# Attention kernel on Trainium2: the inversion of a tile's softmax normalisers moves from VectorE to GpSimd

## What is computed

```python
q = _fq_sym(q, axis=-1); k = _fq_sym(k, axis=-1); v = _fq_sym(v, axis=2)
attn = jnp.einsum('bhqd,bhkd->bhqk', q, k)
attn = jax.nn.softmax(attn.astype(jnp.float32), axis=-1)
attn = _fq_unsigned(attn, axis=-1)      # to 0..255 of the row's largest
out = jnp.einsum('bhqk,bhkd->bhqd', attn, v)
out = out @ Wp + bp
```

## Time and profile before

| what | value |
|---|---|
| median of three runs | 1166.4 us |
| the profiled execution's own time | 1166.14 us |
| its span | 1164.4 us |
| mean granted TensorE clock | 0.994 |
| busy in the span: PE, DVE, ACT, POOL | 90%, 82%, 77%, 60% |
| attention in its steady form | about 130 to 690 us of the span |
| finish of tile 0 and of tile 15 on VectorE | at 136.8 and at 732.7 us |

### The profile page before, as it was taken

How to read it: one execution, slowest core, us unless ns; L and a number is a source line. 1 busy time by engine, 2 the same in 40 slices (tenths; PEclk the granted TensorE clock), 3 DMA queues, 4 the chain that set the end, 5 groups by cost and what they waited for, 6 DMA issues and landing times.

```text
span 1164.4 us, 24047 instructions
## 1 busy us (share of the span) xinstructions
PE 1048.7 (90%) x8281; PEld 606.3 (52%) x8396; DVE 950.6 (82%) x1748; ACT 891.8 (77%) x1546; POOL 701.3 (60%) x625
## 2 busy tenths in 40 slices
PE   8988888888888888888888889899998999999997
PEld 4743444444444444444444447656654465557775
DVE  6999999999999999999999996863336788953335
ACT  4779999999999999999999996734543576834441
POOL 3016888888777878888788776447651000753332
PEclk9999999999999999999999999899999999999999
DMA  6697998888888889888876764856938001523336
GB/s 193 120 163 149 173 172 162 169 169 171 167 172 175 165 166 170 178 162 170 155 118 111 115 109 78 243 170 181 321 115 331 0 1 46 178 84 109 97 97 233
DMA packets 388799, 176.36 MB, mean 151 GB/s; under 512 B 330413, under 2 KB 373650, under 8 KB 388680
## 3 DMA queue, kind: packets, MB, share of 16 engines
q1 hardware_dynamic: 381976, 157.85, 62.1%
q0 software_dynamic: 6480, 16.77, 4.3%
q10 hardware_dynamic: 224, 0.20, 0.1%
HBM read 52.70 MB, written 43.59 MB: 83 GB/s over the span
## 4 chain that ended last, share of the span: by engine, by line
PE 49%; DVE 28%; ACT 13%; issue 5%; DMA 2%; POOL 2%; SPq 1%; ACTq 0%; POOLq 0%; DVEq 0%
DVE top L426 22%; ACT weight L485 10%; PE bank L220 8%; PE bank L234 8%; PE bank L1187 4%; PE bank L2616 4%; PE bank L1580 3%; PE bank L252 3%; PE bank L2632 3%; PE bank L1166 2%; PE bank L1174 2%; PE bank L1853 1%; PE bank L1598 1%; PE bank L682 1%; POOL dispatched_rows L1823 1%
## 5 line engine op out<-in xcount | busy, mean ns | idle before, releaser
L485 ACT ACTIVATE weight<-bank,bias,sq_all 128x1024 uint8<-128x1024 f32 x512 | 609.9, 1201 | 24.0 <-PE bank L234 18.7
L426 DVE TENSOR_REDUCE top<-bank 128x1 f32<-128x512 f32 (+1 forms) x683 | 610.2, 951 | 11.5 <-PE bank L220 1.1
L537 POOL CAST weight<-turned 128x2048 bf16<-128x2048 uint8 x256 | 478.8, 1892 | 41.0 <-PE bank L252 22.2
L234 PE MATMUL bank<-kT,query 128*128 128x512 bf16 x917 | 284.1, 382 | 26.4 <-ACT weight L485 12.2
L252 PEld LDWEIGHTS bank<-v_sb,weight 128*128 128x128 bf16 x4096 | 172.0, 96 | 102.7 <-POOL weight L537 0.5
L220 PE MATMUL bank<-kT,qspace 64*128 64x512 bf16 x687 | 135.0, 387 | 55.8 <-DVE top L426 55.8
L252 PE MATMUL bank<-v_sb,weight 128*128 128x16 bf16 x4096 | 172.6, 170 | 0.8 <-POOL weight L537 0.4
L220 PE MATMUL bank<-kT,query 128*128 128x512 bf16 x329 | 124.8, 379 | 2.1 <-DVE top L426 1.4
L234 PEld LDWEIGHTS bank<-kT,query 128*128 128x128 bf16 x1024 | 59.9, 97 | 103.9 <-ACT weight L485 61.9
L1823 POOL DMA_INDIRECT dispatched_rows<-qspace,put x32 | 37.1, 1160 | 116.0 <-DVE qspace L2373 106.9
L485 ACT ACTIVATION_READ_ACCUMULATOR weight<-bank,bias,sq_all 128x1 f32 x512 | 101.7, 199 | 0.0
(11 more groups left out here) (352 smaller groups left out, 1471.7 us busy)
## 6 DMA issues: line engine op xcount, KB each, us to landing
dispatched_rows<-zeros SPq DMA_DIRECT2D x32, 524.0 KB, 3.1
answered_rows<-zeros SPq DMA_DIRECT2D x16, 512.0 KB, 3.2
late<-answered_rows SPq DMA_DIRECT2D x16, 512.0 KB, 6.3
erow<-dispatched_rows SPq DMA_DIRECT2D x39, 131.0 KB, 2.1
wgu<-in_L_ffn_w_gate SPq DMA_DIRECT2D x26, 176.0 KB, 3.8
wgu<-in_L_ffn_w_up SPq DMA_DIRECT2D x26, 176.0 KB, 3.7
query<-qspace SPq DMA_DIRECT2D x32, 128.0 KB, 3.1
turned<-weight SPq DMA_TRANSPOSE x256, 3.1
```

The source lines that it names most:

```text
L234: mm = pe.matmul(unit[u % 2][:, v * 512:(v + 1) * 512], query2[:, t % 2, h, :], kT[:, h // 2, first + v * 512:first + (v + 1) * 512], star ...
L426: ve.tensor_reduce(top[:, first:first + count], bank[:, first % 3:first % 3 + count, :], AX.X, ALU.max).then_inc(s_max, 1)
L485: ac.activation(weight8[:, n % BYTES, u * 1024:(u + 1) * 1024], unit[u], ACT.Exp, bias=bias[:, n:n + 1], scale=sq_all[:, n:n + 1], accum_o ...
L537: po.tensor_copy(weight[:, n % 3, :, :, :].rearrange("p c q two -> p (c q two)"), turned8[:, n % 3, :, :].rearrange("p c q -> p (c q)").bi ...
```

## The change

GpSimd gets a second instruction a tile: behind the addition of the halves it waits for that addition, and then raises the 16 sums to the power of minus one in place, with a tile of constants as exponents. That tile is filled once, in the preparation. The semaphore `s_rn`, for which VectorE and ScalarE wait, now counts the powers and not the sums. VectorE's reciprocal and its wait for it are left out.

```diff
+            inverse = sa("inverse", [P, H])
@@ finish_tile (VectorE)
                 ve.wait_ge(s_rn, t + 1)
-                ve.reciprocal(rnorm[:, t % 2, :], rnorm[:, t % 2, :]).then_inc(s_rnv, 1)
-                ve.wait_ge(s_rnv, t + 1)
                 ve.wait_ge(s_val, H * (t + 1))
                 ve.tensor_tensor(attn[:, t, :].rearrange("p (h d) -> p h d", h=H),
@@ attention_pool (GpSimd), behind the cast of head 15
                         po.wait_ge(s_exp, 2 * (n + 1))
-                        po.tensor_tensor(rnorm[:, t % 2, :], norm[:, t % 2, :, 0], norm[:, t % 2, :, 1], ALU.add).then_inc(s_rn, 1)
+                        po.tensor_tensor(rnorm[:, t % 2, :], norm[:, t % 2, :, 0], norm[:, t % 2, :, 1], ALU.add).then_inc(s_sums, 1)
+                        po.wait_ge(s_sums, t + 1)
+                        po.tensor_tensor(rnorm[:, t % 2, :], rnorm[:, t % 2, :], inverse[:], ALU.pow).then_inc(s_rn, 1)
@@ prepare_pool (GpSimd)
                     step(po.memset(eps_rms[:], RMS_EPS))
+                    step(po.memset(inverse[:], -1.0))
```

More of the change, by code:

```diff
@@ L177, in program @@
             s_wide, s_val = sem("weights_widened"), sem("head_values_summed")
-            s_ofree, s_rn, s_rnv = sem("tile_outputs_taken"), sem("normalisers_added"), sem("normalisers_inverted")
+            s_ofree, s_sums, s_rn = sem("tile_outputs_taken"), sem("normalisers_added"), sem("normalisers_inverted")
             s_q2 = [sem(f"padded_queries_copied_{k}") for k in range(2)]
```

## The result

The changed kernel takes 1168.2 us (median of 22 runs, 1164.8 to 1171.5) against 1166.4 us for the kernel before (22 runs, 1163.5 to 1167.6). The ratio is 1.0018, with a 95% interval of 1.001 to 1.0026: slower by a little, 1.8 us, where 4.4 us faster was forecast. The profiled execution took 1167.14 us, its span is 1165.4.

The account below looks back on a forecast made before the run. VectorE's list was taken to bound finish rounds, a chain through TensorE the ordinary ones. Terms -4.2 - 0.2 + 0 = -4.4 us gave 1162.0 us against 1166.4; range 1160.6 to 1167.5.

Parts of the forecast that it names:

- What bounds the kernel: Attention's loop: VectorE's list alone sets the 4.10 us finish round; a chain through TensorE holds the ordinary 3.63 us round.
- The reciprocal on VectorE, 15 x 0.28 us: Finish rounds of tiles 0 to 14: removing reciprocal and wait saves 0.28 us each, whole, 4.2 us in all.
- The 0.2 us for the last tile: Tile 15's finish: 0.28 us earlier stays possible before TensorE's product is needed; counted as 0.2 us saved.
- The length of the power: GpSimd's new instruction, absent from the trace: taken as 0.85 us, bounded by 0.214 and 2.27 us.
- What its lateness costs: Casts queued behind the power on GpSimd: delay absorbed by idle time and cover, cost 0; at 2.27 us, 3 us in all.
- (b): Reciprocal in attention was covered after all; the next round gives back the gain: -1.6 us, 1164.8 us; chance 0.14.
- (d): Power on GpSimd above 3.7 us makes VectorE wait at the multiplication; at 5 us, +16 us, 1182.8; chance 0.13.
- (c): Power on GpSimd of 2.3 to 3.7 us eats 3 us of the 4.4 us saving: 1165.0 us; chance 0.07.
- the upper price of 2.27 us: Power priced at GpSimd's dearest elementwise instruction: head 3's cast 1.0 to 1.7 us late, up to 0.2 us a tile.
- (e): First power alone, in tile 0, costs much more, making VectorE wait once: -0.7 us left, 1165.7 us; chance 0.04.

Follow-up runs that it names:

- The kernel with the product: Changed kernel with GpSimd's power replaced by a same-shape product with a constant (1/420), true inverse left out: 1161.9 us, ratio 0.9962 to the kernel before.
- 1.9 us of work: Changed kernel with the power taken of heads 8 to 15 alone, a product with a constant for heads 0 to 7: 1160.5 us, attention 548.5 us.
- the fourth slot: Changed kernel with four slots of turned bytes in place of three, so a transpose waits for the cast of four heads back: 1166.0 us.
- 2.5 us of work: Changed kernel with the power taken of heads 4 to 15, a product with a constant for heads 0 to 3: 1167.15 us, attention 552.4 us.

## Why the prediction was wrong, point by point

- What bounds the kernel: right. The finish round is VectorE's own, others are held by a loop through TensorE.
- The reciprocal on VectorE, 15 x 0.28 us: right in place and size. The kernel with the product gives 4.5 us, 4.0 of them over the 14 tiles of the stretch. Of the changed kernel's finish rounds, ten are at 3.80 or 3.81 us, forecast 3.82. The 0.2 us for the last tile isn't seen: from the multiplication of tile 14 to the end it is 475.6 us before and with the product, and the kernel with the inverse on ScalarE, which keeps the reciprocal of tile 15, is as fast as that with the product.
- The length of the power: the step that failed first. I took 0.85 us, and as an end 2.27 us, from GpSimd's dearest elementwise row ahead of 760 us. That was no bound of an operation which the trace doesn't have; behind 760 us the same trace has even a plain addition of 8 elements that took 1.21 us. It is 2.93 us, by the six shapes run 0.42 us and 0.157 us an element ((2.93 - 0.576) / 15), some 75 times the 2 ns that an element of an addition adds. With a power of 0.85 us the forecast would most likely have held, as 1.9 us of work still cost only 0.9.
- What its lateness costs: the step that failed second. I named the idle time ahead of the biases and the cover of the first cast. The cover that decides is that of the casts behind the first, 2.6 us at the second in tile 12 and 1.8 in tile 0, and I read no row of them. I also wrote that transposes shift with the casts and three slots cover that; the fourth slot shows 2.2 us of cost. At the upper price of 2.27 us I had a loss of 3 us; at 2.5 us of work it is 4.7, and at the real length 7.1 (6.3 by the medians), which is more than the whole saving.
- Rivals: (b) falls with the product. (d) had the sign right, but not the mechanism: VectorE waits nowhere for the power. It is (c) that happened, late casts with a power between 2.3 and 3.7 us, which I gave a chance of 0.07 and a loss of 3 us. It eats more than all of the 4.4 us. Its sign was to be TensorE waiting for casts of heads 3 to 7; the waits start at head 1. The range ended at 1167.5 because I priced that mechanism at no more than 3 us.
- A first power dearer than the rest (e): no. All 16 in the changed kernel (shortest, median, longest in ns):

```profile
L545 POOL TENSOR_TENSOR rnorm<-rnorm,inverse x16: 2928/2929/2944, 132.7 to 731.8; 128x16 f32<-128x16 f32 x16
```

  The Trainium skill's 6 us for the first call of freshly loaded code ("GPSIMD Engine Reference", "Instruction dispatch") isn't seen here: the first power starts 0.29 us behind the start of its sum, as the one at 293.24 does.
- The Trainium skill's advice to keep elementwise additions, products and maxima on VectorE ("GPSIMD Engine Reference", "Engine selection") turns out right for the inverse too, but its factor of about two is not stated for a power: the inverse takes 2.93 us on GpSimd and 0.24 us on VectorE, twelve times as long. I had used the factor to say that the sum would stay the same.

Left open: why the long rounds away from a finish fall where they do (behind the finishes of tiles 1, 2, 4, 5 and 9 in the changed kernel), how much of them is late casts and how much slow landings of transposes, and why the runs of the changed kernel scatter more (1164.8 to 1171.5 against 1163.5 to 1167.6). Four slots removed about half of these rounds; the rest were not taken apart.

## What to carry to other kernels

Before work is moved to an idle engine, look for the first consumer of each thing that is queued behind it there, not only for the engine's idle time and not only for the first consumer: here there were 3.4 to 3.8 us of cover at the first cast, and 1.8 to 2.6 at the second in the two tiles taken apart. A saving on the engine that bounds a round brings others sooner to their producers, so it takes cover away from work that was added elsewhere; measure both together. And an instruction that costs in a full round may be nearly free in the round before: moving the reciprocal by three reductions gave 3.6 us, without another engine.

## What was not expected of the hardware

- A power on GpSimd costs 0.42 us and 0.157 us for each element of a partition: 0.58, 0.86, 1.35, 1.67, 2.30 and 2.93 us for 1, 3, 6, 8, 12 and 16. A sum of 16 takes 0.21 us, a product 0.22.
- On ScalarE a logarithm or exponential of 128 x 16 is put between two exponentials of 128 x 1024 for 0.10 us of its list.
- On VectorE the reciprocal holds the list for 0.16 us where nothing waits for it, and for 0.28 us where the next instruction does.
